# A GNN kernel's edge sort: the count of a batch from pairwise added one-hot tables, eight products in place of sixteen

## The chip, the cores and the metric

The kernel runs on one core of a Trainium2 chip. The metric is the device time of one execution in microseconds (us); of several executions the median is given. The core has TensorE (PE in the profile; its weight loads are PEld), VectorE (DVE), ScalarE (ACT), GpSimd (POOL) and SyncE (SP, which here only issues DMAs). They run side by side and are ordered by semaphores.

## The reference

Two graph layers over 12500 nodes (256 features) and 200000 edges, which come sorted by `dst`.

```python
# layer 0: H = 4 heads of 32
feat = relu(einsum('nd,ohdk->ohnk', x, W0) + b0)        # self and neighbour features
edge_w = (att_s[:, src] + att_n[:, dst]) * edge_weight
agg = segment_sum(edge_w[..., None] * feat_nei[:, dst], src, N)
x = layernorm(x + concat(norm(feat_self), norm(agg)))
# layer 1
m = relu(concat(x[src], x[dst]) @ W_msg + b_msg)
agg = segment_sum(m, dst, N)
x = layernorm(x + norm(relu(concat(x, agg) @ W_upd + b_upd)))
```

The sum of layer 0 runs over `src`, and the edges are sorted by `dst`. So the kernel first sorts the messages of layer 0 by the 128-row tile of `src`; that stage is where the change lies.

## The kernel before

**Stages.** The first stage, called the sort (profile time 0 to about 790 us), puts the messages of layer 0 into runs by tile and writes them to `d_m`. The second (to about 1925 us) gathers those runs, adds them up by node and does layer 0's norm. The third does the edges and nodes of layer 1.

**The sort** goes over NB = 108 batches. A batch is 116 lanes (partitions) by COLS = 16 columns of edges, and there are NT = 98 tiles of nodes. Each engine has its own `sort(j)`, called for the steps j = 0 to 117 (`sorting`, NB + DEEP steps); each handles several batches in one step, at different ages, so the whole is a software pipeline written out by hand. Each engine works through its instructions strictly in the order written. What matters here, with the batch that is handled in step j:

- VectorE, batch j (L1628): `OHS[j % 4]`, the one-hot table of the batch, 16 columns of 98 tiles each, fp16, 1568 elements a partition, written as a comparison with the tile numbers. It signals `s_oh`. Its other long instructions of a step are L1638 (the tables times the ranks, batch j-3), L1643 (`SELT`, batch j-9), L1651 and L1664 (batch j-5), and L1677.
- TensorE, batch j-1 (L1212): the count. With the strictly upper triangular matrix `utb` as weights it adds up 16 products of 98 columns each, one per column of the batch, into `PS`. That gives, for each lane and tile, how many edges of the lanes before it go to that tile. It signals `s_L`; ScalarE copies the result out (L980).
- TensorE, batch j-10 (`expand`, L1185): 45 products in five groups that select the messages of the batch from the gathered rows `FWN[q % 3]`. Group 0 stands at the head of the step and waits for the gather (`s_fw`) and for `SELT` (`s_od`). Groups 1 to 4 lie between the other jobs. Group 0, one small product, L1205 and group 1 stand ahead of the count.
- GpSimd, in the order of a step: the indirect gather of the rows of batch j-9 from `d_ts` into `FWN` (L772, 128 rows of 792 bytes); three small additions for batch j-10 (L780, L782, L784, 15 or 16 elements a partition), the first of which waits until `MSG` has been stored; a one-column copy for batch j-2 (L788), which waits for ScalarE's L961; in steps 7 to 32 one more indirect gather (L795).
- SyncE, in the order of a step: the load of `NUM` for batch j-8 (L651, 480 KB), a load of `xT`, a store of `d_ts`, the store of 3.8 KB for batch j-7 (L662), and the two stores of `MSG` for batch j-10 (L668, 603 and 402 KB), which wait for GpSimd's small additions (`s_id`) and for ScalarE's evictions (`s_ev`).

In steps 3 to 53 each step also carries one pair of node tiles of layer 0's features (VectorE L1656, L1669, L1682, L1686, L1691; TensorE L1175). After that the steps are shorter.

**The lines that the change touches besides.** `wut` (256 KB, `[128, 2, 256]` fp32) holds a half of the update weights. It is loaded at the start (L626, semaphore `w2`) and used in the third stage only, by `upper` (L1366). The third stage begins with SyncE's loads of `WUB` (L715) and `GM` (L716), and then `spread(0)` (L723), the load for which VectorE's first instruction of the stage waits.

```python
                if 0 <= l < NB:
                    waitn(e, "s_l2", l - 1)
                    waitn(e, "s_oh", l + 1)
                    for cc in range(COLS):
                        m = e.matmul(PS[l % 2][:, 0:NT], utb[L, :], OHS[l % 4][L, cc, :], start=(cc == 0), stop=(cc == COLS - 1))
                    m.then_inc(S("s_L"), 1)
```

Of the kernel before, what the change touches and what calls it, by code (L numbers as in the profile page):

```python
# [7 lines left out]
f16 = mybir.dt.float16  # L8
ALU = mybir.AluOpType
# [5 lines left out]
NT = 98  # L15
# [11 lines left out]
NB = 108  # L27
LANES = 116
COLS = 16
# [196 lines left out]
def gnn(nc, x, xT, src, dst, ew, srcB, dstB, ewB, dst0, W0, b0, att, scale, offset, Wm, bm, Wu, bu, gam, bet, cst, out):  # L226
    ctx = ExitStack()
    with ctx:
        def sb(name, shape, dt=f32):
            return ctx.enter_context(nc.sbuf_tensor(name, shape, dt))  # L230
# [63 lines left out]
        wm = sb("wm", [128, 2, 512])  # L294
        wut = sb("wut", [128, 2, 256])
        bbt = sb("bbt", [128, 256])

# [279 lines left out]
        def _(e):  # L577
# [47 lines left out]
            e.dma_start(wm[:, :, 256:512], Wm[256:512, :].rearrange("(k p) n -> p k n", p=128)).then_inc(s_w, 16)  # L625
            e.dma_start(wut[:, :, :], Wu[0:256, :].rearrange("(k p) n -> p k n", p=128)).then_inc(S("w2"), 16)  # L626
            e.dma_start(bbt[:, :], bet.rearrange("(a n) -> a n", a=1).to_broadcast([128, 256])).then_inc(S("w2"), 16)
# [85 lines left out]
            waitn(e, "d_mm", NP)  # L713

            e.dma_start(WUB, Wu[256:512, :].rearrange("(k p) n -> p k n", p=128)).then_inc(s_w, 16)  # L715
            e.dma_start(GM, gam.rearrange("(a n) -> a n", a=1).to_broadcast([128, 256])).then_inc(s_w, 16)  # L716
# [33 lines left out]
        def _(e):  # L750
# [14 lines left out]

            def sort(j):
                q = j - 9
                if 0 <= q < NB:
# [374 lines left out]
        def _(e):  # L1143
# [50 lines left out]
            def sort(j):  # L1194
# [13 lines left out]
                if 0 <= l < NB:  # L1208
                    waitn(e, "s_l2", l - 1)
                    waitn(e, "s_oh", l + 1)  # L1210
                    for cc in range(COLS):
                        m = e.matmul(PS[l % 2][:, 0:NT], utb[L, :], OHS[l % 4][L, cc, :], start=(cc == 0), stop=(cc == COLS - 1))  # L1212
                    m.then_inc(S("s_L"), 1)
# [69 lines left out]
            e.wait_ge(S("tb"), T_DONE)  # L1283
            e.wait_ge(S("w2"), 32)

# [82 lines left out]
            def node1(p, o):  # L1368
# [16 lines left out]
                if o == 2:  # L1385
                    waitn(e, "g_at", p + 1)
                    if p == 0:
                        e.wait_ge(s_w, 16 * 8)
                    waitn(e, f"g_in{p % 2}", 16 * (p // 2 + 1))
                    for b in range(2):  # L1390
                        v = (PU_END if end else PG)[:, b * 256:(b + 1) * 256]
                        if not end:
                            upper(v, p, b, True)
                        for k in range(2):
                            m = e.matmul(v, AT[:, 2 * b + k, :], WUB[:, k, :], start=False, stop=(end and b == k == 1))  # L1395
                        if not end:
                            m = bias(v, 2)
                    m.then_inc(S("g_mm"), 1)
# [56 lines left out]
        def _(e):  # L1455
# [159 lines left out]
            def sort(j):  # L1615
# [9 lines left out]
                if j < NB:  # L1625
                    waitn(e, "s_L", j - 3)
                    waitn(e, "s_pr", j - 3)
                    e.tensor_tensor(twos(OHS[j % 4][L]), iotaH[L, :].rearrange("p (n t) -> p n t", t=2).unsqueeze(1).to_broadcast(b49),  # L1628
                                    tfp[L, j * COLS:(j + 1) * COLS, :].unsqueeze(2).to_broadcast(b49), ALU.is_equal).then_inc(S("s_oh"), 1)
# [212 lines left out]
            def node(p, o):  # L1842
# [54 lines left out]
                if o == 13:  # L1897
                    waitn(e, "b_nm", 2 * (p + 1))
                    e.tensor_tensor(x1, XN, bc2(bbt[:, :]), ALU.add).then_inc(S("b_xb"), 1)
            e.wait_ge(S("w2"), 32)  # L1900
            for g in range(E_END):
# [45 lines left out]
            def node1(p, o):  # L1947
# [20 lines left out]
                if o == 10:  # L1968
                    if p == 0:
                        e.wait_ge(s_w, 16 * 8)  # L1970
                    waitn(e, "g_n1", 2 * (p + 1))
# [203 lines left out]
```

## Time and profile before

| | |
|---|---|
| median of 3 executions | 4360.93 us (4351.94 to 4366.93) |
| the profiled execution, its own time | 4342.88 us |
| its span, first to last instruction | 4340.9 us |
| busy share of the span | PE 86%, PEld 71%, DVE 76%, ACT 64%, POOL 57% |
| mean granted clock of TensorE | 0.948 of full speed |

In the rows below, a time such as 656.09 is us from the start of the span. "Busy" is the time in which an engine had an instruction running; what stands in square brackets is the engine's idle time before an instruction, and what ended it ("issue": nothing that the profile shows). The mean of a product is its latency; products overlap, so their rate is read from a run of them in the timeline. "x16" is a count of instructions. DMA is the mean busy share of the 16 DMA engines.

### The profile page before, as it was taken

Reading aid. Unit: us, or ns where it says so; the run is one execution under the profiler, and the core shown is the slowest. Engines: PE = TensorE matmul, PEld = TensorE weight load, DVE = VectorE, ACT = ScalarE, POOL = GpSimd, SP = SyncE. Lnnn points to the kernel's source line nnn. Section 1 sums busy time; section 2 is a strip of 40 time slices with the busy share of each in tenths; the row PEclk is TensorE's granted clock in tenths of the full one; section 3 lists DMA queues with packets and bytes.
Section 4 is the critical chain, followed back from the end, with each engine's and each line's share of the span. In section 5 each row is a group of like instructions: output and inputs, shape, how many; then the busy total and the mean of one; then the engine's idle time right before and its main releaser. Section 6 shows DMA issues by size and latency. Waiting matters only on the chain.

```text
span 4340.9 us, 83221 instructions
## 1 busy us (share of the span) xinstructions
PE 3744.9 (86%) x24828; PEld 3084.9 (71%) x24828; DVE 3301.7 (76%) x7638; ACT 2769.9 (64%) x7571; POOL 2465.7 (57%) x2585
## 2 busy tenths in 40 slices
PE   4999999899999999966887888888888888888886
PEld 3889999788888888855666666666666666666665
DVE  7999998699999999955666666666666666666666
ACT  4888888677777777744555555555555556555555
POOL 1554555345555455436666666666666666666663
PEclk8999999899999999988999998999999999999998
DMA  4999888667777777643444444444444444444443
GB/s 127 284 300 299 285 282 280 212 191 210 205 208 207 211 210 209 203 146 115 129 142 129 136 131 133 134 131 135 131 142 131 137 128 138 138 133 133 135 129 93
DMA packets 349890, 754.55 MB, mean 174 GB/s; under 512 B 62337, under 2 KB 192974, under 8 KB 349418
## 3 DMA queue, kind: packets, MB, share of 16 engines
q0 software_dynamic: 114912, 359.18, 29.8%
q1 hardware_dynamic: 234538, 390.01, 27.1%
q8 instruction: 214, 3.51, 0.3%
q14 instruction: 226, 1.85, 0.1%
HBM read 561.05 MB, written 189.53 MB: 173 GB/s over the span
## 4 chain that ended last, share of the span: by engine, by line
PE 35%; DVE 29%; issue 13%; another core or an unknown queue 9%; DMA 7%; ACT 4%; DVEq 2%; SPq 1%; POOL 0%; ACTq 0%; POOLq 0%
PE ps L1348 10%; PE ps L1360 10%; DVE big L1935 8%; PE ps L1326 4%; DVE scr L1785 4%; DVE arena L1945 4%; DMA d_pos<-big 3%; DVE arena L1788 3%; PE ps L1185 2%; DMA arena<-d_m,scr 2%; DVE scr L1788 1%; PE ps L1366 1%; PE ps L1395 1%; DVEq L1935 1%
## 5 line engine op out<-in xcount | busy, mean ns | idle before, releaser
L820 POOL DMA_INDIRECT arena<-d_p,tabs x1612 | 1544.6, 958 | 851.6 <-issue 441.9
L1348 PE MATMUL ps<-arena 128*128 128x256 f32 x3224 | 890.9, 415 | 232.5 <-DVE big L1935 149.5
L1945 DVE TENSOR_TENSOR arena<-arena,ps 128x512 f32<-128x512 f32 x806 | 525.6, 684 | 731.0 <-remote 491.9
L1139 ACT ACTIVATE arena<-arena 128x1024 f32<-128x1024 f32 x403 | 425.6, 1056 | 994.3 <-DVE arena L1945 886.1
L1360 PE MATMUL ps<-big,scr 128*128 x3224 | 837.2, 400 | 209.3 <-DVE arena L1945 130.8
L1348 PEld LDWEIGHTS ps<-arena 128*128 128x128 f32 x3224 | 616.5, 202 | 422.1 <-ACT arena L1139 152.9
L1360 PEld LDWEIGHTS ps<-big,scr 128*128 128x128 f32 x3224 | 637.6, 201 | 348.0 <-issue 253.7
L806 POOL DMA_INDIRECT arena<-d_m,scr x392 | 527.1, 1345 | 577.5 <-DVE arena L1788 254.8
L1935 DVE SCALAR_TENSOR_TENSOR big<-big,tabs,ps 128x256 f32 x1612 | 769.6, 477 | 107.6 <-DVE big L1935 51.9
L1326 PE MATMUL ps<-arena,scr 128*128 128x256 f32 x2620 | 615.1, 384 | 11.2 <-DVE arena L1788 11.1
L1326 PEld LDWEIGHTS ps<-arena,scr 128*128 128x128 f32 x2620 | 484.1, 190 | 93.0 <-issue 33.0
L1024 ACT ACTIVATE arena<-arena 128x128 f32<-128x128 f32 x1310 | 410.8, 389 | 195.7 <-PE ps L1326 131.6
L1092 ACT ACTIVATE arena<-cstb,tabs 128x128 f32<-128x128 f32 x1612 | 508.8, 386 | 2.3 <-DMA d_p<-arena 2.3
L1185 PE MATMUL ps<-arena,scr 128*128 128x132 bf16 x4860 | 372.9, 223 | 11.3 <-issue 7.4
L1785 DVE TENSOR_TENSOR scr<-scr,arena 128x640 f32<-128x640 f32 x392 | 321.1, 819 | 3.3 <-issue 3.1
L1185 PEld LDWEIGHTS ps<-arena,scr 128*128 128x128 bf16 x4860 | 313.7, 99 | 13.7 <-issue 10.9
L1326 PE MATMUL ps<-scr 128*128 128x256 f32 x1300 | 309.1, 385 | 9.9 <-DVE scr L1788 9.8
L935 ACT ACTIVATE arena<-ps 128x396 f32<-128x396 f32 x540 | 259.1, 494 | 32.1 <-PE ps L1185 25.1
L1326 PEld LDWEIGHTS ps<-scr 128*128 128x128 f32 x1300 | 240.6, 191 | 51.5 <-issue 16.4
L1095 ACT ACTIVATE arena<-arena 128x512 f32<-128x512 f32 x403 | 253.8, 630 | 12.8
L1024 ACT ACTIVATE scr<-arena 128x128 f32<-128x128 f32 x650 | 203.8, 389 | 91.1 <-PE ps L1326 64.5
L1788 DVE TENSOR_TENSOR arena<-arena 128x640 f32<-128x640 f32 x262 | 214.7, 819 | 5.8 <-ACT arena L1024 5.6
(292 smaller groups left out, 5387.9 us busy)
## 6 DMA issues: line engine op xcount, KB each, us to landing
d_m<-arena SPq DMA_DIRECT2D x108, 603.0 KB
arena<-d_loc SPq DMA_DIRECT2D x135, 384.0 KB
d_m<-arena SPq DMA_DIRECT2D x108, 402.0 KB
big<-d_pos SPq DMA_DIRECT2D x54, 480.0 KB
tabs<-d_pos SPq DMA_DIRECT2D x54, 480.0 KB
arena<-d_p,tabs POOLq DMA_INDIRECT x1612
arena<-in_xT_dram SPq DMA_DIRECT2D x96, 256.0 KB
d_xp<-arena SPq DMA_DIRECT2D x49, 256.0 KB, 3.3
```

The costliest lines, as they stand in the source:

```text
L806: e.indirect_dma_start(out=GB[g % 4].rearrange("p a b -> p (a b)"), out_offset=None, in_=runs_m, in_offset=bass.IndirectOffsetOnAxis(ap=TI ...
L820: e.indirect_dma_start(out=G1[j % 8][:, k, :], out_offset=None, in_=d_p, in_offset=bass.IndirectOffsetOnAxis(ap=tabS[:, j, k:k + 1], axis= ...
L1024: a = e.activation(SW[g % 3][:, s, 0:128], v[:, 0:128], ACT.Copy, scale=v[:, FW + 1:FW + 2])
L1092: s = e.activation(OH1[j % 4][:, k, :], iota, ACT.Square, bias=tabN[:, j, k:k + 1])
L1139: e.activation(G1[g % 8], G1[g % 8], ACT.Relu).then_inc(S("f_re"), 1)
L1185: m = e.matmul(PS[5 + (NE * q + k) % 3][:, (cc - c0) * FW:(cc - c0 + 1) * FW], SELT[q % 2][:, cc, :], FWN[q % 3][:, i * FW:(i + 1) * FW], ...
L1326: m = e.matmul(AC(p)[:, h, :], OHW[g % 3][:, s, :], SW[g % 3][:, s, :], start=first, stop=end)
L1348: m = e.matmul(turn(H, AB)[:, k * 256:k * 256 + 256], OH1[(j - 2) % 4][:, 2 * h + k, :], G1[(j - 2) % 8][:, 2 * h + k, :], start=True, sto ...
L1360: m = e.matmul(turn(H, QB)[:, k * 256:k * 256 + 256], OT1[j % 2][:, 2 * h + k, :], big[:, ts[2 * h + k] + 1, :], start=True, stop=True)
L1785: e.tensor_tensor(OHW[g % 3], IT[t % 3].unsqueeze(1).to_broadcast(b5), v[:, :, FW].unsqueeze(2).to_broadcast(b5), ALU.is_equal).then_inc(S ...
L1935: e.scalar_tensor_tensor(big[:, ts[k], :], big[:, ts[k], :], tabK[:, j - 3, k:k + 1], turn(H, AB)[:, (k % 2) * 256:(k % 2) * 256 + 256], A ...
L1945: e.tensor_tensor(v, v, q2(turn(2 * j + h, QB)[:, :]), ALU.add).then_inc(S("f_m"), 1)
```

## The change

- GpSimd gets, at the head of each of the steps 0 to 107, one addition: `HS = OHS[j % 4][:, 0:8] + OHS[j % 4][:, 8:16]`, 784 fp16 elements a partition on 116 partitions. It waits for `s_oh` (VectorE's table of batch j) and for `s_L >= j` (TensorE's count of batch j-1, since there is one buffer `HS`). It signals `s_hs`.
- TensorE's count of batch j-1 waits for `s_hs` in place of `s_oh`, and adds up 8 products from `HS` in place of 16 from `OHS`.
- VectorE's L1628 waits for `s_hs` (the addition of batch j-4) in place of `s_L` (its count).
- `HS` lies in `wut`, so the load of `wut` moves from the start to the beginning of the third stage, ahead of `WUB`; the counts of the semaphores `w2` and `s_w` follow.

```diff
--- before.py
+++ after.py
@@ -226,6 +226,9 @@
 def gnn(nc, x, xT, src, dst, ew, srcB, dstB, ewB, dst0, W0, b0, att, scale, offset, Wm, bm, Wu, bu, gam, bet, cst, out):
     ctx = ExitStack()
     with ctx:
+        def grid16(v):
+            return v.bitcast(f16).rearrange("p (a b) -> p a b", b=NT)
+
         def sb(name, shape, dt=f32):
             return ctx.enter_context(nc.sbuf_tensor(name, shape, dt))
 
@@ -293,6 +296,7 @@
         small = sb("small", [128, 4, 112])
         wm = sb("wm", [128, 2, 512])
         wut = sb("wut", [128, 2, 256])
+        HS = grid16(wut[:, :, :].rearrange("p a b -> p (a b)")[:, 0:NT * COLS // 4])
         bbt = sb("bbt", [128, 256])
 
         def carve(buf, start=0):
@@ -623,7 +627,6 @@
             e.dma_start(zero_m[13 * 128:1675, :], zer[0:11, :]).then_inc(S("s_lz"), 16)
             e.dma_start(wm[:, :, 0:256], Wm[0:256, :].rearrange("(k p) n -> p k n", p=128)).then_inc(s_w, 16)
             e.dma_start(wm[:, :, 256:512], Wm[256:512, :].rearrange("(k p) n -> p k n", p=128)).then_inc(s_w, 16)
-            e.dma_start(wut[:, :, :], Wu[0:256, :].rearrange("(k p) n -> p k n", p=128)).then_inc(S("w2"), 16)
             e.dma_start(bbt[:, :], bet.rearrange("(a n) -> a n", a=1).to_broadcast([128, 256])).then_inc(S("w2"), 16)
             e.dma_start(nxt_i[0:124, :], dst[1600:E].rearrange("(p c) -> p c", c=1600)[:, 0:1],
                         allow_slow_non_contiguous=True).then_inc(s_dl, 16)
@@ -712,6 +715,7 @@
             waitn(e, "b_mm", pq(NP, 0))
             waitn(e, "d_mm", NP)
 
+            e.dma_start(wut[:, :, :], Wu[0:256, :].rearrange("(k p) n -> p k n", p=128)).then_inc(s_w, 16)
             e.dma_start(WUB, Wu[256:512, :].rearrange("(k p) n -> p k n", p=128)).then_inc(s_w, 16)
             e.dma_start(GM, gam.rearrange("(a n) -> a n", a=1).to_broadcast([128, 256])).then_inc(s_w, 16)
             e.wait_ge(S("lc"), 32)
@@ -764,6 +768,10 @@
             L = slice(0, LANES)
 
             def sort(j):
+                if j < NB:
+                    waitn(e, "s_oh", j + 1)
+                    waitn(e, "s_L", j)
+                    e.tensor_tensor(HS[L], OHS[j % 4][L, 0:COLS // 2], OHS[j % 4][L, COLS // 2:COLS], ALU.add).then_inc(S("s_hs"), 1)
                 q = j - 9
                 if 0 <= q < NB:
                     k = need(q)
@@ -1207,9 +1215,9 @@
                     expand(x, 1)
                 if 0 <= l < NB:
                     waitn(e, "s_l2", l - 1)
-                    waitn(e, "s_oh", l + 1)
-                    for cc in range(COLS):
-                        m = e.matmul(PS[l % 2][:, 0:NT], utb[L, :], OHS[l % 4][L, cc, :], start=(cc == 0), stop=(cc == COLS - 1))
+                    waitn(e, "s_hs", l + 1)
+                    for cc in range(COLS // 2):
+                        m = e.matmul(PS[l % 2][:, 0:NT], utb[L, :], HS[L, cc, :], start=(cc == 0), stop=(cc == COLS // 2 - 1))
                     m.then_inc(S("s_L"), 1)
                 if 0 <= x < NB:
                     expand(x, 2)
@@ -1281,7 +1289,7 @@
             e.matmul(PS[6][:, 32:33], ones[0:NB, :], ovs[0:NB, :], start=True, stop=False)
             e.matmul(PS[6][:, 32:33], ones[0:125, :], flag[0:125, :], start=False, stop=True).then_inc(S("tp"), 1)
             e.wait_ge(S("tb"), T_DONE)
-            e.wait_ge(S("w2"), 32)
+            e.wait_ge(S("w2"), 16)
 
             def own(j, o):
                 if o == 0:
@@ -1385,7 +1393,7 @@
                 if o == 2:
                     waitn(e, "g_at", p + 1)
                     if p == 0:
-                        e.wait_ge(s_w, 16 * 8)
+                        e.wait_ge(s_w, 16 * 9)
                     waitn(e, f"g_in{p % 2}", 16 * (p // 2 + 1))
                     for b in range(2):
                         v = (PU_END if end else PG)[:, b * 256:(b + 1) * 256]
@@ -1623,7 +1631,7 @@
                     waitn(e, "s_c", q)
                     e.tensor_reduce(RKP[L], grid(PS[2][L, 0:7 * COLS], 7), AX.X, ALU.add).then_inc(S("s_rk"), 1)
                 if j < NB:
-                    waitn(e, "s_L", j - 3)
+                    waitn(e, "s_hs", j - 3)
                     waitn(e, "s_pr", j - 3)
                     e.tensor_tensor(twos(OHS[j % 4][L]), iotaH[L, :].rearrange("p (n t) -> p n t", t=2).unsqueeze(1).to_broadcast(b49),
                                     tfp[L, j * COLS:(j + 1) * COLS, :].unsqueeze(2).to_broadcast(b49), ALU.is_equal).then_inc(S("s_oh"), 1)
@@ -1897,7 +1905,7 @@
                 if o == 13:
                     waitn(e, "b_nm", 2 * (p + 1))
                     e.tensor_tensor(x1, XN, bc2(bbt[:, :]), ALU.add).then_inc(S("b_xb"), 1)
-            e.wait_ge(S("w2"), 32)
+            e.wait_ge(S("w2"), 16)
             for g in range(E_END):
                 if g < NGA:
                     edge0(g)
@@ -1967,7 +1975,7 @@
                                            sm(p, rc, 2), ALU.mult, ALU.mult).then_inc(S(names[2]), 1)
                 if o == 10:
                     if p == 0:
-                        e.wait_ge(s_w, 16 * 8)
+                        e.wait_ge(s_w, 16 * 9)
                     waitn(e, "g_n1", 2 * (p + 1))
                     e.tensor_tensor(u, u, bc2(GM), ALU.mult).then_inc(S("g_gm"), 1)
                 if o == 11:
```

## Rows read from the trace of the kernel before

**Rows 1.** Windows, first and third stage: busy PE, PEld, DVE, ACT, POOL; PEclk, DMA.

```profile
0.00:800.00 800.00, 695.97 (x11061) 651.95 (x11061) 687.51 (x1434) 630.67 (x2104) 397.24 (x583) 0.96 0.81 265
1925.00:4341.00 2416.00, 1962.71 (x7975) 1523.31 (x7975) 1551.68 (x3605) 1336.55 (x2904) 1544.59 (x1612) 0.92 0.44 131
```

**Rows 2.** Windows of the sort, VectorE's L1628 alone: busy (count), PEclk, DMA, GB/s.

```profile
0.00:180.00 180.00, 19.36 (x20) 0.89 0.64 187
180.00:440.00 260.00, 35.91 (x37) 0.99 0.92 298
440.00:740.00 300.00, 49.62 (x51) 1.00 0.83 283
```

**Rows 3.** Windows of the sort's two halves, all engines, columns as above.

```profile
180.00:440.00 260.00, 251.50 (x3905) 233.69 (x3905) 245.66 (x539) 225.94 (x770) 141.17 (x198) 0.99 0.92 298
440.00:740.00 300.00, 288.20 (x5048) 277.01 (x5046) 269.71 (x518) 261.70 (x929) 175.64 (x260) 1.00 0.83 283
```

**Rows 4.** Timeline, VectorE: L1628 of two successive steps, first half of the sort.

```profile
404.75 0.97 DVE L1628 TENSOR_TENSOR arena<-big 116x1568 f16<-116x1568 f16 x1
...
411.54 0.96 DVE L1628 TENSOR_TENSOR tabs<-big 116x1568 f16<-116x1568 f16 x1
```

**Rows 5.** Timeline, VectorE, one step of the second half.

```profile
656.09 0.96 DVE L1628 TENSOR_TENSOR tabs<-big 116x1568 f16<-116x1568 f16 x1
...
657.08 0.96 DVE L1638 TENSOR_TENSOR tabs<-arena,big 116x1568 f16<-116x1568 f16 x1
659.45 0.72 DVE L1643 TENSOR_SCALAR scr<-tabs,cstb 128x1920 bf16<-128x1920 bf16 x1 [1.42 <-DMA tabs<-d_pos]
...
662.80 0.96 DVE L1628 TENSOR_TENSOR arena<-big 116x1568 f16<-116x1568 f16 x1
```

**Rows 6.** Timeline, TensorE, the step beside it.

```profile
654.78 0.70 PE L1185 MATMUL ps<-arena,scr 128*128 128x132 bf16 x9
...
656.19 0.89 PE L1212 MATMUL ps<-tabs,big 116*128 116x98 f16 x16
...
660.32 0.70 PE L1185 MATMUL ps<-arena,scr 128*128 128x132 bf16 x9
```

**Rows 7.** Timeline, GpSimd: the gather of batch 85, and a small addition.

```profile
652.41 1.21 POOL L772 DMA_INDIRECT arena<-d_ts,arena  x1 [0.34 <-issue]
...
657.10 1.02 POOL L782 TENSOR_TENSOR big<-arena 128x16 f32<-128x16 f32 x1
```

**Rows 8.** Windows: gathers L772 begun by 653, and products L1185 begun by 660.3.

```profile
0.00:653.00 653.00, 104.88 (x86) 0.97 0.81 263
0.00:660.30 660.30, 294.81 (x3825) 0.97 0.81 263
```

**Rows 9.** Groups by form, GpSimd: its short fp16 write, mean ns of one.

```profile
L758 POOL TENSOR_SCALAR scr<-cstb 128x128 f16<-128x128 f32 x4 | 2.0, 527 | 0.6 <-DMA cstb<-in_cst_dram 0.6
```

**Rows 10.** Timeline, GpSimd and VectorE: a small addition, and L1677 beside it.

```profile
662.22 0.22 POOL L780 TENSOR_TENSOR arena<-arena 128x15 f32<-128x15 f32 x1 [1.92 <-DMA d_m<-arena]
...
662.25 0.45 DVE L1677 TENSOR_TENSOR big<-big 116x240 f16<-116x240 f16 x1
```

**Rows 11.** Timeline, GpSimd and VectorE: the conversion L763, and L1506 beside it.

```profile
13.36 2.60 POOL L763 CAST big<-big 116x1728 f16<-116x1728 int32 x1 [1.47 <-DVE big L1504]
...
13.32 1.06 DVE L1506 TENSOR_SCALAR arena<-arena 116x1728 int32<-116x1728 int32 x1
```

**Rows 12.** The chain that ended last, the sort's end: the gather of batch 106.

```profile
772.37 5.71 DMA arena<-d_ts,arena
```

**Rows 13.** DMA issues by line; last column: median us from issue to landing.

```profile
wut<-in_L_gnn_W_upd_dram SPq DMA_DIRECT2D x1, 256.0 KB, 3.9
...
cstb<-in_cst_dram SPq DMA_DIRECT2D x1, 255.0 KB, 2.7
```

**Rows 14.** Timeline of SyncE; the chain: where wut's load leaves and where it goes.

```profile
39.05 0.52 SPq L626 DMA_DIRECT2D wut<-in_L_gnn_W_upd_dram  x1
...
1924.99 5.91 issue
```

## The prediction

> **What bounds the kernel now.** I read the windows by stage first. The sort fills the first 790 us; the third stage, 2416 us with TensorE at 81%, is touched by the change only where it begins [rows 1]. So the sort's step is the thing to price. The windows with VectorE's L1628 alone count steps, since it runs once in each: 37 steps in 260 us, 7.03 us a step, while the node tiles ride along, then 51 steps in 300 us, 5.88 us a step [rows 2]. In both halves TensorE is 97 and 96% busy, VectorE 94 and 90%, GpSimd 54 and 59% [rows 3]. Seen as shares, TensorE is the one to relieve and GpSimd the one with room.
>
> The timelines say more. In the first half VectorE goes from one L1628 to the next in 6.79 us [rows 4]; its instructions between them follow each other without idle time, so it bounds that half. In the second half its step takes 6.71 us here with 1.42 us idle, so 5.29 us of work [rows 5]. TensorE's step beside it is 5.54 us, from group 0 of one batch to group 0 of the next (654.78 to 660.32), without a gap, and there it is the bound most of the time [rows 6].
>
> The third thing to see is how early GpSimd is with its gather. The one that starts at 652.41 is the 86th, batch 85 [rows 7, 8]. By 660.3 TensorE has begun 3825 products of `expand`, which is 85 batches of 45, so the group that starts at 660.32 is batch 85's. The gather is 7.9 us ahead of its use. It can be, because nothing in GpSimd's step waits for something late in TensorE's.
>
> **The change part by part.**
>
> *TensorE* loses 8 of the 16 products of a count. The 16 take 0.89 us together [rows 6]; the latency of the last doesn't halve, so I take 0.4 us a step off, between 0.35 and 0.45. At most that is 108 x 0.4 = 43 us, and only where TensorE is the bound.
>
> *GpSimd's addition.* No addition of this length is in the trace. Nearest above: L758, 128 elements in 527 ns [rows 9], less the 0.22 us that a 15-element addition takes [rows 10], is 2.4 ns an element, so 784 x 2.4 + 220 ns = 2.1 us. Nearest below: the conversion L763, one input, 1728 elements in 2.60 us. It begins at 13.36, and VectorE's L1506 beside it ends at 14.38; if that kept it waiting, 1.58 us are left, 0.91 ns an element, so 784 elements cost 0.71 + 0.22 = 0.93 us [rows 11]. The addition has two inputs to read, so I take twice that rate: 1.43 + 0.22 = 1.65 us. The Trainium skill (GPSIMD Engine Reference, Elementwise — side-by-side cycle accounting) gives about 2.6 cycles of 1.2 GHz for an element of a two-input addition, which would be about 1.7 us for 784, an estimate from that page.
>
> *What it does to VectorE.* A GpSimd addition of 16 elements beside L1638 took 1.02 us, until 658.12, just behind L1638's end at 658.04 [rows 5, 7]: such operations wait for a VectorE instruction that reads two tensors. So the addition waits up to 0.97 us; I take 0.4. The other way round the rows show little: L1677 took 0.45 us beside a 0.22 us addition [rows 10]. VectorE may lose nothing, or the whole 1.65 us a step. I take nearly all of it, since four long instructions of its step read two tensors and only one can slip past. The Trainium skill (SBUF — State Buffer, Who interferes with whom) has the rule that a VectorE instruction with two SBUF inputs and a GpSimd one that reads SBUF hold the shared port for their whole length, whoever starts first; the waiting GpSimd rows agree, and no row shows VectorE held by a long addition. By that rule the first half's step is at least 7.03 + 1.65 = 8.7 us; without it VectorE alone leaves it at 7.0.
>
> *What it does to the gather.* This is the largest term. The addition stands at the head of GpSimd's step and waits for the count of batch j-1, which TensorE does in step j. Behind it in the queue stands the gather of batch j-9, which TensorE wants at the head of step j+1. The lead of 7.9 us is gone, and a ring closes, once a step: count, addition, gather, landing, group 0 and group 1, count. Its length:
> - hand-over from the count, 0.3 us (an estimate from the 0.34 us of issue before the gather [rows 7])
> - wait for the port, 0.4 (0 to 0.97)
> - addition, 1.65 (0.93 to 2.1)
> - issue before the gather, 0.35 [rows 7]
> - gather, from its start to its landing: 5.71 us at the sort's end [rows 12]. The lowest that any load of some size took is 2.7, `cst`, at the quiet start [rows 13]. The DMA engines are now 83 to 92% busy in the sort [rows 3]; over a longer step the same bytes leave them 60 to 75% busy, and the stores of `MSG`, which wait for GpSimd's small additions, are now issued behind the gather and not ahead of it. I take 4.0, between the ends
> - from the start of group 0 to the end of the count, 657.08 - 654.78 = 2.30 [rows 6], less 0.4: 1.9
>
> The sum is 8.6 us. The rest of TensorE's step (3.2 us) lies beside it and costs nothing.
>
> *SyncE's queue.* The stores of `MSG` wait for the small additions, which stand behind the gather; they land two steps before ScalarE needs the buffer, so they aren't late. VectorE's L1628 waits for an addition three steps old: nothing.
>
> *The load of `wut`* leaves the start, where its issue took 0.52 us of SyncE's queue, and goes to where VectorE waits 5.91 us for the load behind it [rows 14]. The issue and up to the 3.9 us of its transfer [rows 13] could stand there; most of it overlaps, I take 1.5 - 0.5 = +1 us.
>
> *TensorE's clock.* It would be idle 8.6 - 5.1 = 3.5 us in each step, 60% busy. In the third stage, at 81% busy, the granted clock was 0.92, in the sort's second half 1.00 [rows 1, 3]. At 0.9 the 1.9 us become 2.1, some 20 us in all. I leave it out of the sum and keep it for the high end.
>
> **Sum.** First half: two bounds, 8.6 and 8.7, so close that I take 8.8: 37 x (8.8 - 7.03) = 65. Second half: 51 x (8.6 - 5.88) = 139. The first 180 us hold 20 steps, 9 of which have no gather: 11 x 1.7 = 19. With `wut` +224 us, on 4342.88 us of the profiled execution. That one lies 18 us below the median, so I forecast 4360.93 + 224 = 4585 us; as case A's own range 4520 to 4650. Each 0.1 us on the ring is 10 us.
>
> **The rivals.**
>
> *B: the gather lands in time, and only the port costs.* If the landing is quick (2.7 us) the ring is 7.3 us and VectorE sets the first half. By VectorE's steps: 37 x 1.65 + 51 x (5.29 + 1.65 - 5.88) + 11 x 1.65 = 61 + 54 + 18 = 133, so 4494 us. With an addition of 0.93 us the ring is 6.6 us: 37 x 0.93 + 51 x 0.7 + 11 x 0.93 = 80, so 4441. For it: the stores now come behind the gather. Against it: 5.71. The mechanism is the port rule of the page named above.
>
> *C: the landing stays what it is.* With 5.7 us the ring is 10.3 us: 37 x 3.3 + 51 x 4.4 + 11 x 3.2 = 381, so 4742 us. For it: the load of `NUM` and the stores of the step before are still in the queues. Against it: less traffic for each us.
>
> *D: faster.* TensorE's relief shows in the second half, where it bounds: 51 x 0.4 = 20, so 4341 us. The ring would have to be within 5.1 us, and as it is 4.6 us without the landing, the gather would have to land in 0.5 us. No load does [rows 13].
>
> *E: nothing happens.* The sort stays at what other engines set, and the ring just fits into 5.9 us: a landing of 1.3 us. 4361 us.
>
> **How the numbers follow.** A 0.60, B 0.15, C 0.19, D 0.03, E 0.03. The range goes from the low end of B, 4440, to C with a little of the clock, 4750; D, E and the tails of A and C are left out. Within 0.3% is what a measurement of this kernel can't tell from no change, about 13 us. D gives faster 0.03, E the same 0.03, A, B and C slower 0.94.
>
> **What would show it.** Right: L1628 comes every 8 to 9 us in 440 to 740; TensorE's group 0 of `expand` waits 3 us or more in most steps, released by the gather; L772 starts behind the addition, some 2.5 us after the count. The addition shows 1.6 to 2.6 us. VectorE has either long instructions of twice their length or idle time beside the addition. The stages behind the sort keep their lengths. Wrong: group 0 waits for `SELT` or VectorE (B, or a load of `NUM` that is late), or the steps stay at 5.9 us with the addition below 1 us (E). A sort that ends before 790 us would make the whole argument false.

## The result and the profile after

| | before | after |
|---|---|---|
| median | 4359.9 us (4 executions, 4351.94 to 4366.93) | 4546.08 us (4 executions, 4543.08 to 4549.26) |
| profiled execution, span | 4340.9 us | 4542.3 us |

The ratio is 1.0425 (95% interval 1.0407 to 1.0443): 186 us slower. The page of the changed kernel: span, busy time of each engine, and the rows of GpSimd and of the granted clock in 40 slices.

```profile
span 4542.3 us, 81708 instructions
...
PE 3788.6 (83%) x23964; PEld 3115.9 (69%) x23964; DVE 3458.3 (76%) x7638; ACT 2780.2 (61%) x7571; POOL 2691.1 (59%) x2693
...
POOL 3775677744455555443666666666666666666663
PEclk7999988889999999997989999999998999999898
```
GpSimd has 225 us more, nearly all in the first eight slices, and in slices 6 to 9 the granted clock is down to 0.8. The first product behind the sort's last `expand`, one of the preparation of the second stage, tells how much of the loss is in the sort. First before, then after:

```profile
790.31 0.38 PE L1260 MATMUL ps<-cstb,big 98*108 98x98 f32 x2
```
```profile
965.75 0.38 PE L1268 MATMUL ps<-cstb,big 98*108 98x98 f32 x2
```
That is 175.4 us of the 186. The medians' other 11 us I can't place: in these two profiled executions the third stage is 26 us longer after the change, but the one before was itself 17 us below its median, and single executions of the kernel before are 15 us apart. What the moved load does there is tried below.

The windows of the two stretches of [rows 2], with L1636, which was L1628: 30 steps in 260 us, 8.67 us a step, and 38 in 300 us, 7.89 us, where it was 7.03 and 5.88.

```profile
180.00:440.00 260.00, 28.96 (x30) 0.93 0.79 249
440.00:740.00 300.00, 37.29 (x38) 0.90 0.64 215
```
All engines in the same stretches, against [rows 3]: TensorE falls from 97 and 96% busy to 83 and 78%, VectorE stays at 95 and 88%, the DMA engines fall to 79 and 64%.

```profile
180.00:440.00 260.00, 214.66 (x2981) 196.78 (x2979) 248.16 (x453) 189.64 (x632) 169.92 (x196) 0.93 0.79 249
440.00:740.00 300.00, 234.43 (x3465) 220.32 (x3462) 264.65 (x411) 203.10 (x701) 206.63 (x229) 0.90 0.64 215
```
**One turn of the ring.** The timeline of TensorE, where L1193 is `expand` (it was L1185) and L1220 the count (L1212):

```profile
702.96 1.17 PE L1193 MATMUL ps<-arena,scr 128*128 128x132 bf16 x9 [2.38 <-DMA arena<-d_ts,arena]
...
705.39 0.78 PE L1220 MATMUL ps<-wut,big 116*128 116x98 f16 x8
...
711.48 0.71 PE L1193 MATMUL ps<-arena,scr 128*128 128x132 bf16 x9 [1.90 <-DMA arena<-d_ts,arena]
...
712.99 0.86 PE L1220 MATMUL ps<-wut,big 116*128 116x98 f16 x8
```
GpSimd in the same stretch, L774 the addition and L780 the gather:

```profile
706.32 1.68 POOL L774 TENSOR_TENSOR wut<-tabs 116x784 f16<-116x784 f16 x1 [3.15 <-PE ps L1220]
708.15 1.51 POOL L780 DMA_INDIRECT arena<-d_ts,arena  x1 [0.15 <-issue]
...
714.00 1.85 POOL L774 TENSOR_TENSOR wut<-tabs 116x784 f16<-116x784 f16 x1 [1.92 <-PE ps L1220]
```
The count ends at 706.17 (705.39 + 0.78). The addition starts 0.15 us later and takes 1.68, the gather starts at 708.15, TensorE has waited 1.90 us for it when group 0 starts at 711.48, 3.33 us after the gather, and the next count ends at 713.85, 2.37 us further. 0.15 + 1.68 + 0.15 + 3.33 + 2.37 = 7.68 us, the distance from count to count. The next addition starts 0.15 us after it again. Nothing in this circle has slack.

VectorE in the same stretch (L1672 was L1664, L1668 was L1660), beside the two additions:

```profile
706.50 2.31 DVE L1672 TENSOR_TENSOR big<-big 116x1536 bf16<-116x1536 bf16 x1
...
714.25 1.76 DVE L1668 TENSOR_TENSOR big<-big 116x256 bf16<-116x256 bf16 x1
716.04 0.96 DVE L1672 TENSOR_TENSOR big<-big 116x1536 bf16<-116x1536 bf16 x1
```
An instruction of 0.96 us takes 2.31, and the short one behind, 0.28 us elsewhere, takes 1.76. VectorE is stopped for 1.35 and 1.48 us.

The chain that ended last, by line, from 540 to 840 us; then who waited for whom from 540 to 900 us (total us, times, longest):

```profile
by line: DMA arena<-d_ts,arena 40.0%; issue 23.2%; PE ps L1193 18.5%; POOL wut L774 7.4%; PE ps L1220 6.3%; PE ps L1213 2.7%; PE ps L1200 2.1%; POOLq L250 0.4%
```
```profile
POOL wut L774 <- PE ps L1220: 96.1, 46, 4.3
PEld ps L1193 <- DMA arena<-d_ts,arena: 88.4, 45, 3.7
PE ps L1193 <- DMA arena<-d_ts,arena: 81.9, 45, 3.6
```
What the chain contains is the ring: the gather's landing 40%, the two groups of `expand`, the two small products, the count, the addition, and the hand-overs ("issue" also holds the part of an addition in which it waited for the port). VectorE isn't in it. Of 46 steps, 45 wait for the gather, 1.8 us each on the mean (81.9 / 45 for the products).

### The profile page after: what moved, and what is told of

Same layout as the page of the kernel before. It is cut to its first block, busy times and chain, and to the rows that moved or that the text cites. A ratio compares the mean times of both kernels' runs of the same rounds, so it can differ in the third digit from the quotient of the medians.

```text
span 4542.3 us, 81708 instructions
## 1 busy us (share of the span) xinstructions
PE 3788.6 (83%) x23964; PEld 3115.9 (69%) x23964; DVE 3458.3 (76%) x7638; ACT 2780.2 (61%) x7571; POOL 2691.1 (59%) x2693
## 4 chain that ended last, share of the span: by engine, by line
PE 34%; DVE 26%; issue 14%; DMA 10%; another core or an unknown queue 10%; ACT 3%; DVEq 2%; POOL 1%; SPq 1%; POOLq 0%; ACTq 0%
PE ps L1356 10%; PE ps L1368 9%; DVE big L1943 7%; DMA arena<-d_ts,arena 7%; PE ps L1334 4%; PE ps L1193 3%; DVE arena L1953 3%; DVE scr L1793 3%; DVE arena L1796 2%; DMA arena<-d_m,scr 2%; PE ps L1374 1%; POOL wut L774 1%; DVE scr L1796 1%; PE ps L1403 1%
## 5 line engine op out<-in xcount | busy, mean ns | idle before, releaser
L1356 PE MATMUL ps<-arena 128*128 128x256 f32 x3224 | 900.7, 420 | 210.8 <-DVE big L1943 148.3
L1356 PEld LDWEIGHTS ps<-arena 128*128 128x128 f32 x3224 | 628.0, 206 | 401.3 <-ACT arena L1147 161.9
L1193 PE MATMUL ps<-arena,scr 128*128 128x132 bf16 x4860 | 415.9, 238 | 172.9 <-DMA arena<-d_ts,arena 168.1
L1193 PEld LDWEIGHTS ps<-arena,scr 128*128 128x128 bf16 x4860 | 347.5, 107 | 188.2 <-DMA arena<-d_ts,arena 182.0
L774 POOL TENSOR_TENSOR wut<-tabs 116x784 f16<-116x784 f16 x81 | 178.2, 2200 | 214.9 <-PE ps L1220 163.7
```

The lines of the kernel that those rows point to most:

```text
L1193: m = e.matmul(PS[5 + (NE * q + k) % 3][:, (cc - c0) * FW:(cc - c0 + 1) * FW], SELT[q % 2][:, cc, :], FWN[q % 3][:, i * FW:(i + 1) * FW], ...
L1356: m = e.matmul(turn(H, AB)[:, k * 256:k * 256 + 256], OH1[(j - 2) % 4][:, 2 * h + k, :], G1[(j - 2) % 8][:, 2 * h + k, :], start=True, sto ...
```

## The experiments

The third stage depends on the chip: it takes 2416 us in the profile of the kernel before and 2073 in that of `load_moved`, on another chip, and the kernel before took 4360 or 4354 us in two sets of executions and 4001 or 3998 in two others. So differences are taken against the kernel before on the same chip. Beside them stands the time at which the sort's last `expand` ends in the profiled execution. Between two profiles of one and the same sort it differs by 9 to 15 us (790 us before and 775 in `load_moved`, which has the same sort; 966 and 975 in the changed kernel), so smaller differences of it say nothing.

**The changed kernel again.** The same file, on another chip.

> The changed kernel itself, beside the others of this call, because the third stage differs by some 350 us from chip to chip (4360 and 4001 us for the kernel before). The sort should end where it did, at about 966 us, and the difference to the kernel before should again be about 186 us, whatever the ratio.

Measured: 4187.26 us against 3998.35, ratio 1.0467 (1.0451 to 1.0482), 188.9 us. The loss in us is that of the first chip, since it lies in the sort.

**The gather in front of the addition.** GpSimd's four lines of the addition move behind the gather:

```diff
-                if j < NB:
-                    ...
-                    e.tensor_tensor(HS[L], ...).then_inc(S("s_hs"), 1)
                 q = j - 9
                 if 0 <= q < NB:
                     ...
                     e.indirect_dma_start(out=FWN[q % 3], ...)
+                if j < NB:
+                    waitn(e, "s_oh", j + 1)
+                    waitn(e, "s_L", j)
+                    e.tensor_tensor(HS[L], ...).then_inc(S("s_hs"), 1)
```

> The changed kernel, but with GpSimd's addition written behind the gather of its step, so that the gather no longer stands behind the wait for the count. Ring theory with VectorE stopped by the addition (mine): the gather leads its use again by about a step, group 0 no longer waits for it, and VectorE sets the step: 5.29 + 1.66 = about 7.0 to 7.2 us in the second half (7.82 now), about 8.5 in the first (8.63 now); 4500 us, some 45 below the changed kernel. Ring theory alone (VectorE loses nothing): steps return to 7.0 and 5.8 us or less, 4320 to 4365 us. Port theory alone (the ring costs nothing): no difference, 4546 us.

Measured: 4129.01 us against 4001.33, ratio 1.0314 (1.0289 to 1.0338): 127.7 us, 61 less than the change. The second half's step (L1636 from step 53 to 107) is 6.91 us in place of 7.82; the first half's hardly moves, 8.33 against 8.63. Of the three forecasts only that of the mixed theory, ring and stopped VectorE, is near; the ring alone would give no loss, the port alone the whole 186 us. What I hadn't expected is the landing. GpSimd, SyncE (L671 the stores of `MSG`, L654 the load of `NUM`) and TensorE around one gather:

```profile
706.69 1.65 POOL L776 DMA_INDIRECT arena<-d_ts,arena  x1 [0.34 <-issue]
```
```profile
706.25 1.47 SPq L671 DMA_DIRECT2D d_m<-arena  x2
707.82 0.41 SPq L654 DMA_DIRECT2D tabs<-d_pos  x1
```
```profile
714.19 0.71 PE L1193 MATMUL ps<-arena,scr 128*128 128x132 bf16 x9 [1.48 <-DMA arena<-d_ts,arena]
```
The gather starts at 706.69, 0.44 us behind the issue of the 1 MB of stores, and its use at 714.19 still waited for it: 7.45 us to landing, with DMA engines that are only 71% busy on the mean of 440 to 740 us. In the 3 us behind the start of this gather they are 90% busy:

```profile
706.69:709.69 3.00, 3.00 (x57) 2.82 (x55) 2.94 (x6) 2.41 (x10) 1.90 (x2) 1.00 0.90 340
```
So the gather again holds up the expansion in part of the steps, by another way.

**Two buffers.** The order stays, but `HS` has two buffers, so the addition may start a step earlier. 

```diff
-                    waitn(e, "s_L", j)
-                    e.tensor_tensor(HS[L], OHS[j % 4][L, 0:COLS // 2], ...
+                    waitn(e, "s_L", j - 1)
+                    e.tensor_tensor(HS[j % 2][L], OHS[j % 4][L, 0:COLS // 2], ...
```

`wut`, 16 columns and `bbt` become one tensor of 784 columns that holds both, and `bbt` is loaded behind the sort.

> The changed kernel, order as it is, but with two buffers for the added tables, so that the addition of batch j waits for the count of batch j-2 and not j-1 (the tensor bbt is loaded behind the sort to make the room). The ring then spans two steps. Ring theory with VectorE stopped: as with the gather first, 4490 to 4520 us, second-half step 7.0 to 7.3 us. Ring alone: 4320 to 4365 us. Port alone: 4546 us.

Measured: 4116.01 us against 4001.33, ratio 1.0287 (1.0264 to 1.0309): 114.7 us. The same windows as above:

```profile
180.00:440.00 260.00, 29.93 (x31) 0.97 0.82 258
440.00:740.00 300.00, 42.22 (x44) 0.95 0.73 243
```
44 steps in 300 us, 6.8 us a step, a little below the 7.0 to 7.3 that I had expected. The second buffer takes off 74 us of the 189; the two losses are from two chips, so 74 is good to some 10 us.

**The addition alone.** The count takes 16 products from VectorE's tables again; the addition is made, waits for no count, and nobody reads it.

```diff
-                    waitn(e, "s_L", j)
+                    waitn(e, "s_hs", j)
                     e.tensor_tensor(HS[L], ...
...
-                    waitn(e, "s_hs", l + 1)
-                    for cc in range(COLS // 2): ... HS[L, cc, :]
+                    waitn(e, "s_oh", l + 1)
+                    for cc in range(COLS): ... OHS[l % 4][L, cc, :]
...
                     waitn(e, "s_hs", j - 3)
+                    waitn(e, "s_L", j - 3)
```

> The changed kernel with the count of 16 products straight from VectorE's tables, as before, and with the addition still made in the same place but waiting for no count, and read by nobody. This leaves GpSimd's addition as the only load. If the addition stops VectorE for its whole length: first half 8.5 us a step, second half 7.0 to 7.3 us, 4500 us. If it stops nobody: 4360 us. If VectorE loses part of it, in between in proportion.

Measured: 4112.82 us against 4001.33, ratio 1.0281 (1.0258 to 1.0303): 111.5 us, where 140 were expected; the sort ends at 892 us. The chain by line from 540 to 840 us has hardly any TensorE and 2% of landings; it goes through GpSimd:

```profile
by line: issue 47.4%; POOL arena L780 17.4%; POOL arena L792 13.2%; POOL wut L774 8.2%; POOL big L796 4.3%; POOL arena L788 3.4%; POOL big L790 3.2%; DMA arena<-d_ts,arena 2.1%; POOLq L250 0.5%; PE ps L1193 0.3%
```
That view follows semaphores, and in it VectorE's stops and GpSimd's waits for the port don't show as waits: the addition takes 2.41 us in the median in place of 1.66, and that counts as work or as "issue". The window of all engines says who sets the step:

```profile
440.00:740.00 300.00, 257.60 (x4291) 243.71 (x4290) 296.86 (x460) 230.45 (x798) 232.92 (x264) 0.98 0.73 242
```
VectorE is busy for 296.86 of the 300 us, where it was 269.71 before [rows 3]. Its 5.29 us of work and the stop of 1.41 us that is measured below are 6.70, and the steps 53 to 107 are 6.71 us long.

TensorE does 16 products here and 8 in `two_buffers`, and the two are 3 us apart, within their intervals. So the halved count is worth nothing that shows where VectorE sets the step.

**Half the addition.** As the last, with 392 elements:

```diff
-                    e.tensor_tensor(HS[L], OHS[j % 4][L, 0:COLS // 2], OHS[j % 4][L, COLS // 2:COLS], ALU.add)
+                    e.tensor_tensor(HS[L, 0:4], OHS[j % 4][L, 0:4], OHS[j % 4][L, 4:8], ALU.add)
```

> As port_only (count of 16 products, addition unread and waiting for no count), but the addition has 392 elements in place of 784, so about 0.85 us in place of 1.66. If VectorE is stopped while GpSimd reads: half of port_only's loss, a sort that ends at about 840 us (790 before, 892 in port_only). If the loss is a fixed price for each GpSimd operation that meets VectorE: as port_only, 892 us.

Measured: 4048.02 us against 3998.35, ratio 1.0119 (1.0104 to 1.0133): 49.7 us, somewhat less than half of 111.5; sort to 828 us. That fits the stop that lasts as long as GpSimd's operation, and not a fixed price.

**A write in place of the addition.**

```diff
-                    e.tensor_tensor(HS[L], OHS[j % 4][L, 0:COLS // 2], OHS[j % 4][L, COLS // 2:COLS], ALU.add)
+                    e.memset(HS, 0.0)
```

> As port_only, but in place of the addition GpSimd writes zeros over the same 784 elements: it waits for the same signal, takes about as long as the half addition (0.8 us), and reads nothing. The Trainium skill (SBUF - State Buffer, Who interferes with whom) says that a two-input VectorE instruction contends only with a GpSimd instruction that reads SBUF. By that, VectorE's two-input instructions keep their 0.96 us and the sort ends at 790 to 800 us. If any long GpSimd operation stops VectorE: about 840 us, like the half addition.

Measured: 4021.94 us against 3998.35, ratio 1.0054 (1.0039 to 1.0068): 23.6 us, sort to 809 us. All three operations become ready when `s_oh` comes. An addition then waits for L1647 (which was L1638) to end, and L1652 behind it (`SELT`, which was L1643) bears the stop. L1652's shortest, median and longest ns with the whole addition, the half and the write:

```profile
L1652 DVE TENSOR_SCALAR scr<-big,cstb x54: 720/2126/2136, 105.8 to 882.7; 128x1920 bf16<-128x1920 bf16 x54
L1652 DVE TENSOR_SCALAR scr<-tabs,cstb x54: 719/2126/2135, 114.0 to 888.4; 128x1920 bf16<-128x1920 bf16 x54
```
```profile
L1652 DVE TENSOR_SCALAR scr<-big,cstb x54: 719/1383/1390, 102.8 to 817.5; 128x1920 bf16<-128x1920 bf16 x54
L1652 DVE TENSOR_SCALAR scr<-tabs,cstb x54: 719/1383/1389, 110.7 to 823.1; 128x1920 bf16<-128x1920 bf16 x54
```
```profile
L1652 DVE TENSOR_SCALAR scr<-big,cstb x54: 703/712/832, 100.4 to 798.5; 128x1920 bf16<-128x1920 bf16 x54
L1652 DVE TENSOR_SCALAR scr<-tabs,cstb x54: 709/714/839, 108.1 to 804.3; 128x1920 bf16<-128x1920 bf16 x54
```
It takes 1.41 us longer than 0.72 with 784 elements and 0.66 with 392. The additions themselves last 1.66 and 0.93 us at the shortest, so the stop is the length of the addition less about a quarter of a us. The write doesn't wait, so it runs beside L1647 and is over before L1652; whether a write would stop L1652, which has one input, wasn't tried, and so these runs don't tell whether L1652 is stopped by what GpSimd reads or by any long operation of it. The write of GpSimd runs from 604.20 to 604.95; VectorE beside it:

```profile
604.20 0.75 POOL L774 MEMSET wut<- 128x784 f16 x1 [1.31 <-DVE tabs L1637]
```
```profile
604.13 0.97 DVE L1647 TENSOR_TENSOR tabs<-arena,big 116x1568 f16<-116x1568 f16 x1
605.01 0.72 DVE L1652 TENSOR_SCALAR scr<-tabs,cstb 128x1920 bf16<-128x1920 bf16 x1
```
L1647, with two inputs, starts 0.07 us before the write and ends after it, and keeps its 0.97 us. Of the 108 writes 105 meet L1647, which never takes more than 0.98. The Trainium skill (SBUF — State Buffer, Who interferes with whom) says that a two-input VectorE instruction contends with a GpSimd instruction that reads SBUF and not with one that only writes it, and the trace agrees. The write costs 23.6 us all the same, where I had said 0 to 10. The waits from 440 to 740 us suggest a cause:

```profile
POOL wut L774 <- DVE tabs L1637: 60.8, 37, 3.8
...
PEld ps L1193 <- DMA arena<-d_ts,arena: 21.0, 26, 1.7
```
At the head of its step GpSimd waits for VectorE's table, the gather stands behind that wait, and TensorE comes to wait 21 us for the gather. In `load_moved`, with no such wait, TensorE's list of waits has none for the gather. So a wait at the head of this queue seems to have a price even if what follows it is cheap; a run with the wait and no write wasn't made.

**Sixteen products on the ring.** The changed kernel with all waits, but the count from 16 products:

```diff
-                    for cc in range(COLS // 2): ... HS[L, cc, :]
+                    for cc in range(COLS): ... OHS[l % 4][L, cc, :]
...
                     waitn(e, "s_hs", j - 3)
+                    waitn(e, "s_L", j - 3)
```

> The changed kernel with the addition and all its waits kept, but the count again of 16 products from VectorE's tables. Ring theory: the count lies on the ring, so each step is 0.36 to 0.5 us longer than in the changed kernel (at half clock up to 0.7), 99 steps: 4580 to 4600 us. If VectorE sets the step instead: no difference from 4546 us.

Measured: 4213.19 us against 4001.33, ratio 1.0528 (1.0499 to 1.0558): 211.9 us, 23 more than the change's 188.9. It goes the way the ring demands, by about half of the 34 to 54 us, though the two losses are from two chips and 23 us is not much more than their intervals together. From the start of group 0 to the end of the count the median of the steps 54 to 106 is 2.31 us against 1.96, so the 0.35 are there. On the mean it is 2.59 against 2.31, with a granted clock in the second half of 0.95 where the changed kernel has 0.90; the addition with its wait and the landing are 0.12 shorter together, and the whole circle is 8.01 us against 7.85:

```profile
440.00:740.00 300.00, 36.72 (x38) 0.95 0.64 213
```
**Both cures.** The addition behind the gather, and two buffers.

> GpSimd's addition behind the gather of its step and with two buffers, both at once: nothing of the ring is left, and the gather waits for neither the count nor VectorE's table of its step. If what is left of the loss is VectorE stopped for 1.4 us a step, it stays: about 100 us above the kernel before, as two_buffers and port_only. If it was still the gather's lateness in part, 60 us or less.

Measured: 4463.42 us against 4353.54, ratio 1.0258 (1.0241 to 1.0275): 109.9 us. No ring is left, and the loss is that of `port_only`; L1652 takes 2.13 us in nearly every step, and VectorE is busy for 297.73 of the 300 us from 440 on. The gather stands behind no wait here, and the loss is not smaller: with VectorE setting the step, the wait at the head of GpSimd's queue costs nothing that shows.

**VectorE adds, second half only, then throughout.** No GpSimd addition, two buffers, the addition behind L1628 in VectorE's own queue; `JV` is 54 in the first kernel and 0 in the second:

```diff
+                if JV <= j < NB:
+                    waitn(e, "s_oh", j + 1)
+                    waitn(e, "s_L", j - 1)
+                    e.tensor_tensor(HS[j % 2][L], OHS[j % 4][L, 0:COLS // 2], OHS[j % 4][L, COLS // 2:COLS], ALU.add).then_inc(S("s_hs"), 1)
```

> The same eight-product count, but VectorE makes the addition itself, into two buffers, behind its L1628, and only for batches 54 to 107; the earlier batches are counted with 16 products as before. There is no GpSimd addition and no ring. 784 fp16 elements should take VectorE about 0.55 us (half of L1628's 0.96 for 1568, and its fixed part). VectorE's work in the second half becomes 5.29 + 0.5 = 5.8 us, TensorE's 5.14. If TensorE is the bound of the second half, the sort is up to 20 us shorter; if the engines are as close as the rows say, VectorE takes over at 5.8 us: no change or up to 15 us slower.

> The same for all 108 batches. In the first half VectorE has no idle time, so each of its steps is 0.5 us longer: 15 to 35 us slower than the kernel before, of which 15 to 20 in the first half. Rival: TensorE's relief of 0.4 us is worth more than that, no change or faster.

Measured: 4356.13 us against 4353.54, ratio 1.0012 (1.0000 to 1.0025), and 4369.68 us, ratio 1.0053 (1.0036 to 1.0071). The addition takes VectorE 0.57 us:

```profile
L1639 DVE TENSOR_TENSOR wut<-tabs x81: 566/567/586, 16.8 to 736.6; 116x784 f16<-116x784 f16 x81
L1639 DVE TENSOR_TENSOR wut<-arena x27: 566/568/569, 53.8 to 742.3; 116x784 f16<-116x784 f16 x27
```
With it in the second half alone the step there is 5.78 us, without it 5.81; throughout, the first half's step goes from 7.28 to 7.49. The window of the first kernel shows why nothing is gained:

```profile
440.00:740.00 300.00, 273.81 (x4684) 260.93 (x4682) 296.39 (x574) 258.97 (x941) 204.05 (x261) 1.00 0.84 285
```
TensorE is busy for 273.81 us in place of 288.20, VectorE for 296.39 in place of 269.71: VectorE has taken over as the bound, at the 5.8 us that were expected. This is the best place for the addition that was tried, and it doesn't beat the kernel before.

**Only the load moved.**

```diff
-            e.dma_start(wut[:, :, :], Wu[0:256, :]...).then_inc(S("w2"), 16)
...
+            e.dma_start(wut[:, :, :], Wu[0:256, :]...).then_inc(s_w, 16)
             e.dma_start(WUB, Wu[256:512, :]...).then_inc(s_w, 16)
```

> The kernel before with nothing but the load of wut moved to the beginning of the third stage. Part of the change by itself. Mine: between 0 and +2 us, not to be told from none. Rival: the transfer delays the first load of the third stage by its whole 3.9 us, +4 us.

Measured: 3999.63 us against 3998.35, ratio 1.0006 (0.9992 to 1.0019). Not to be told from nothing.

## Why the prediction came out as it did

Forecast 4585 us with a range of 4440 to 4750, measured 4546: the way and the place were right, the size was 224 us against 186.

- **The ring** is shown. It is closed in nearly every step, the chain is made of it, and the two cures that open it, each by itself, take 61 and 74 us off. The circle's parts, as means over the steps 54 to 106, worked out from the starts, ends and landings in the trace: hand-over 0.15 (I took 0.3), wait for the port and addition 2.05 (0.4 + 1.65), hand-over 0.15 (0.35), landing 3.14 (4.0), to the start of group 0 0.05, to the end of the count 2.31 (1.9). That is 7.85 us; my sum was 8.6. For the steps 15 to 52 it is 0.19 + 2.35 + 0.15 + 3.56 + 0.09 + 2.22 = 8.56, where I had 8.8. What the ring costs beyond the stopped VectorE lies nearly all in the second half: the steps of `port_only` take 8.37 and 6.71 us, those of the changed kernel 8.63 and 7.82.
- **The landing** is the term that was mis-sized: 3.14 us where I took 4.0, and it is more than all of the 0.75 us by which the ring was too long. I had two reasons for taking less than 5.71, less busy DMA engines and the stores of `MSG` behind the gather. The mean load doesn't tell it: at 71% in `gather_first` the median of the steps 54 to 106 is 6.1 us, at 64% in the changed kernel 3.2. Nor does the order in GpSimd's queue: in `port_memset` too the gather stands ahead of the additions that release the stores, and it lands after 5.0 us. What goes with the landing is how much is still in the queues when the gather starts, worked out from the trace of the steps 54 to 106. The last store of `MSG` was issued 4.6 us before the gather in the changed kernel, 3.6 in `port_only`, 1.1 in `port_memset` and 0.4 in `gather_first` (medians), the DMA engines are 35, 62, 92 and 92% busy in the 3 us behind its start (means), and it lands after 3.2, 3.5, 5.0 and 6.1 us. So on this reading both reasons were right and together worth more than I gave them: TensorE's late count holds the gather back until the stores before it have mostly drained. For the gather at 708.15 of the turn above:

```profile
708.15:711.15 3.00, 1.43 (x29) 1.28 (x26) 3.00 (x6) 1.60 (x6) 2.98 (x3) 1.00 0.16 42
```
  No run varies this alone.
- **TensorE's part** was 0.4 us too short, because the clock was left out of the sum. The median of the stretch is 1.96 us, near the 1.9. Of the 53 turns 28 had the whole clock and took 1.95 us on the mean, and ten had about half of it (0.50 to 0.57) and took 3.17; TensorE had been idle for 1.3 us before the one kind and 2.5 before the other, on the mean. For example, group 0 takes 1.17 us at 702.96 and 0.71 at 711.48. The windows of the two (columns as in the rows of all engines) show a granted clock of half in the one (1.2 of the 2.4 GHz) and the whole in the other; there it falls later, and over that turn to the end of its count it is 0.77:

```profile
702.60:705.90 3.30, 2.94 (x27) 2.63 (x28) 1.85 (x4) 1.47 (x6) 0.57 (x1) 0.50 0.89 327
711.00:712.70 1.70, 1.22 (x17) 1.04 (x18) 0.88 (x2) 0.48 (x2) 1.00 (x3) 1.00 0.00 0
```

- **The addition** itself was right. Its durations:

```profile
L774 POOL TENSOR_TENSOR wut<-tabs x81: 1664/2282/3917, 16.9 to 903.2; 116x784 f16<-116x784 f16 x81
L774 POOL TENSOR_TENSOR wut<-arena x27: 1665/2282/3564, 53.9 to 910.5; 116x784 f16<-116x784 f16 x27
```
  The shortest is 1.66 us against my 1.65. The median of 2.28 holds its wait for VectorE. Against the 392 elements, which take 0.93 at the shortest, it is 1.9 ns an element and 0.2 us fixed, where I had 1.83 and 0.22.

  The Trainium skill (GPSIMD Engine Reference, Elementwise — side-by-side cycle accounting) has about 2.6 cycles of 1.2 GHz for an element of a two-input addition, an estimate of 1.7 us for this one; the trace agrees with 1.66.
- **VectorE stopped nearly for the whole of it** was right: 1.41 us of 1.66. As a bound by itself it gives 111 us, where rival B had 133. In the second half B's 5.29 us plus the stop is what was measured, 6.71.
- **Rival C**, the landing of before, is ruled out by the 3.2 us. **Rival D**, the gain, is ruled out in GpSimd's form by the ring, and in VectorE's form by 1.0012. `two_buffers` and `port_only` say that the 8 products saved bring nothing that shows while GpSimd adds. **Rival E**, no change, is ruled out by the 186 us.
- **The signs.** GpSimd's gather behind the addition, some 2.4 us after the count, VectorE's instructions of twice their length and the wait for the gather came as told. Two were too strong: L1628 comes every 7.8 us in the second half and not every 8 to 9, and group 0 waits 1.8 us on the mean and not 3 or more, since the landing is shorter and TensorE's own step, at the lower clock, longer than the 5.1 us that I had.
- **The second half**: I took 8.6 - 5.88 for 51 steps, 139 us; by the windows it is 7.89 - 5.88, 103 us. These 36 us are nearly all of the 38 between forecast and result; in the first half I had 65 us, and the windows give 37 x (8.67 - 7.03) = 61.
- **The load of `wut`**: +1 us, measured none.

## What to carry to other kernels

In a pipeline written out by hand an engine with 40% idle time isn't free: ask what stands behind the new wait in its queue, and who wants that and how soon. One operation with one buffer between two engines, put in front of a gather that the first of them needs next, closes a ring through both engines and the DMA, and the ring's length, landing included, becomes the step. Where the new work can't be kept off another engine's port, opening the ring gives only part back; here 61 to 79 us of 189.

## What the runs showed of the hardware

- A GpSimd addition stopped VectorE's next instruction for 1.41 us with 784 fp16 elements and for 0.66 with 392, about a quarter of a us less than the addition's own 1.66 and 0.93. A GpSimd write of 0.75 us beside a two-input VectorE instruction left it at 0.97.
- The profiled duration of a GpSimd operation holds its wait for the port: 2.41 us in the median of `port_only` for an addition that takes 1.66.
- A gather of 100 KB landed after 3.2 us (median) when it started 4.6 us behind the last 1 MB of stores, and after 6.1 us when it started 0.4 us behind them, though the DMA engines were about as busy on the mean of the stretch (64 and 71%); in the 3 us behind its start they were 35 and 92% busy.
- TensorE, idle for 1.8 us on the mean before group 0 in each step of 7.8 us, was granted 0.90 of its clock on the mean of the second half where it had 1.00 before. The same TensorE work took 1.95 us in the turns with the whole clock and 3.17 in those with about half of it.
